# Fewer, larger copies of constant rows between two on-chip tiles, in a gated cross-attention and expert kernel

## The reference

```
x = x + tanh(g_xattn) * attention(layernorm(x), ctx, ctx)   # 16 heads of 8, scores + mask row + window mask
x = x + tanh(g_ffn) * experts(layernorm(x))                 # top 2 of 8 experts, silu(x w1) * (x w3) -> w2
```

## Time and profile before

| | |
|---|---|
| three runs | 480.2, 482.2, 482.57 us (median 482.2) |
| the profiled execution | 482.57 us, its span 480.9 us |
| PE busy | 417.2 us (87%) |
| DVE busy | 304.4 us (63%) |
| POOL busy | 259.4 us (54%) |
| ACT busy | 233.7 us (49%) |
| mean granted TensorE clock | 0.965 |
| DMA traffic | 46.24 MB, mean 96 GB/s |

### The profile page before, as it was taken

How to read it: one execution, slowest core, us unless ns; L and a number is a source line. 1 busy time by engine, 2 the same in 40 slices (tenths; PEclk the granted TensorE clock), 3 DMA queues, 4 the chain that set the end, 5 groups by cost and what they waited for, 6 DMA issues and landing times.

```text
span 480.9 us, 14461 instructions
## 1 busy us (share of the span) xinstructions
PE 417.2 (87%) x4569; PEld 365.3 (76%) x4570; DVE 304.4 (63%) x833; ACT 233.7 (49%) x504; POOL 259.4 (54%) x318
## 2 busy tenths in 40 slices
PE   1878699998888989889688988999999999999980
PEld 0555478777676767667468888999899999999970
DVE  3986878877887878788657345764444554554520
ACT  3778245666565555555364544443344444444430
POOL 5753603214655373737175566777666465565561
PEclk9989989999999899999889998999999999999995
DMA  8945545455655464667573334433544333333326
GB/s 220 282 102 99 93 78 86 90 82 82 118 80 116 64 120 73 120 167 205 183 211 84 96 50 52 61 52 59 77 69 56 53 50 44 49 44 44 27 23 185
DMA packets 74783, 46.24 MB, mean 96 GB/s; under 512 B 8608, under 2 KB 71490, under 8 KB 74562
## 3 DMA queue, kind: packets, MB, share of 16 engines
q1 hardware_dynamic: 59072, 34.84, 33.4%
q0 software_dynamic: 12272, 8.92, 14.1%
q10 hardware_dynamic: 3392, 1.88, 1.6%
HBM read 18.12 MB, written 14.20 MB: 67 GB/s over the span
## 4 chain that ended last, share of the span: by engine, by line
PE 62%; DVE 13%; issue 7%; ACT 5%; DMA 5%; SPq 3%; POOL 1%; ACTq 1%; DVEq 0%; POOLq 0%
PE ps_scores L1594 23%; PE ps_max_scores L1602 12%; PE ps_max_scores L780 6%; PE ps_values L826 6%; PE ps_scores L812 3%; DVE rsplit L1063 3%; DMA sums_scratch<-yt,xg 3%; PE ps_max_scores L762 3%; PE ps_scores L762 2%; DVE qkf L521 1%; PE ps_values L1586 1%; DMA bk_col<-in_L_xattn_bk_dram 1%; ACT xn L448 1%; SPq L1542 1%; DVE ed L1133 1%
## 5 line engine op out<-in xcount | busy, mean ns | idle before, releaser
L1715 POOL DMA_INDIRECT sums_scratch<-yt,xg x71 | 115.0, 1619 | 69.2 <-DMA sums_scratch<-yt,xg 30.3
L1594 PE MATMUL ps_scores<-xgT,qs 128*128 128x128 f32 x1136 | 141.2, 278 | 5.2 <-ACT xgT L1640 3.9
L1594 PEld LDWEIGHTS ps_scores<-xgT,qs 128*128 128x128 f32 x1136 | 134.0, 194 | 6.9 <-ACT xgT L1640 4.5
L1681 DVE TENSOR_TENSOR qs<-qs,ps_scores 128x512 f32<-128x512 f32 x71 | 48.8, 687 | 90.9 <-PE ps_scores L1594 71.7
L1063 DVE TENSOR_REDUCE rsplit<-ps_max_scores 128x4 f32<-128x512 f32 x128 | 85.2, 687 | 26.2 <-PE ps_max_scores L762 25.3
L1289 POOL DMA_INDIRECT expert_rows_scratch<-xr,pos x64 | 66.4, 1038 | 25.3 <-issue 13.4
L1602 PE MATMUL ps_max_scores<-w_all,qs 128*128 x568 | 75.9, 277 | 2.4 <-ACT yt L1651 1.7
L974 ACT ACTIVATE pT<-ps_scores 128x1024 f32<-128x1024 f32 x64 | 65.2, 1020 | 19.0 <-PE ps_scores L762 19.0
L1602 PEld LDWEIGHTS ps_max_scores<-w_all,qs 128*128 128x128 f32 x568 | 69.0, 192 | 4.3 <-issue 4.2
L1644 ACT ACTIVATE qs<-ps_scores 128x512 f32<-128x512 f32 x71 | 42.4, 597 | 32.3 <-PE ps_scores L1594 32.3
L780 PE MATMUL ps_max_scores<-ks,qs 121*128 121x128 bf16 x512 | 51.5, 227 | 6.4 <-DVE rsplit L1063 3.5
(11 more groups left out here) (187 smaller groups left out, 532.4 us busy)
## 6 DMA issues: line engine op xcount, KB each, us to landing
qs<-w_all SPq DMA_DIRECT2D x96, 64.0 KB
ks<-w_all SPq DMA_DIRECT2D x96, 64.0 KB
w_all<-in_L_ffn_w_dram SPq DMA_DIRECT2D x24, 256.0 KB
xg<-expert_rows_scratch SPq DMA_DIRECT2D x71, 65.0 KB, 1.9
xs<-in_x_dram SPq DMA_DIRECT2D x4, 512.0 KB, 5.3
sums_scratch<-xs SPq DMA_DIRECT2D x8, 256.0 KB, 4.1
sums_scratch<-yt,xg POOLq DMA_INDIRECT x71, 3.3
expert_rows_scratch<-fill SPq DMA_DIRECT2D x16, 65.0 KB
```

The source lines that it names most:

```text
L1594: ins = nc.tensor.matmul(bank[u % 2][:, c * P:(c + 1) * P], w13[:, u % 2, n, c * P:(c + 1) * P], xgT[:], start=True, stop=True)
L1681: nc.vector.tensor_tensor(hidT[:, u % 2], act_s[:, u % 2], ps_b[u % 2], ALU.mult).then_inc(hid_ready, 1)
L1715: pool.indirect_dma_start(out=z_d, out_offset=bass.IndirectOffsetOnAxis(ap=xg_u[:, u, X_IDX:X_IDX + 1], axis=0), in_=yt[:, u % YRING], in_ ...
```

## The change

The spans copied from tile 0 to tile 1 are put together: fewer and larger ones that cover the same rows. `at` is ROWS_K (57) for `qs` and ROWS_K + PARTS (60) for `ks`; the span 121-124 of `ks` is added at L290 as before.

```
-        STAY_ROWS = tuple(tuple((at, at + QUART) for at in WIN_AT) + tuple((at + QUART, at + ROWS_W) for at in WIN_AT)
-                          + ((at, WIN_AT[1]),) for at in (ROWS_K, ROWS_K + PARTS))
-        TILE_COPIES = 2 * 5 + 1
+        STAY_ROWS = tuple(((WIN_AT[0], ROWS_W), (at, WIN_AT[1] + ROWS_W)) for at in (ROWS_K, ROWS_K + PARTS))
+        TILE_COPIES = 2 * 2 + 1
```

## The result

The change makes the kernel slower: 497.67 us median of four runs (496.59 to 498.1) against 482.1 (480.2 to 482.57), a ratio of 1.0327 (95% interval 1.0294 to 1.0359). The forecast was 494.0, with a range of 487 to 508. The profiled execution took 498.06 us, its span 496.3.

A forecast was written before the change was run, and what follows sets the result against it. TensorE, busy 87% of the span, was taken to bound the kernel. 482.57 + 10.3 (late first L780) + 1.5 (clock) = 494.4 us; with the median 0.4 lower, the forecast was 494.0, range 487 to 508.

The forecast's parts named there:

- Six issues fewer: SyncE's copies cut from 11 issues to 5: group 0's loads could start 6 us earlier, at 25.3 us, worth 0.
- 0.69 us a row: Time for one engine to move a 16 KiB row; the 37 rows then run from 24.9 to 50.4 us.
- 10 x 0.69 = 6.9 us for the rows ahead: Rows of the first three copies on the lone engine before the 37 rows, from near 18 to 24.9 us.
- The queue: SyncE issues two loads during the 37-row copy, the other 11 after it; first L780 comes 10.3 us late.
- 7.0 + 2.4 us behind the copy: After the 37-row copy ends: 7.0 us for 11 load issues, 2.4 us to landing; first half lands at 59.8 us.
- the deep queue: Rival: all 13 loads queue during the copy, leaving one engine's backlog; 5.4 us late at least, 488 us; chance 0.10.
- What is late next: After group 0's first half: group 1's slacks of 9.6 and 10.5 us cover some 4; later stages run as before.
- The clock, 1.5 us: TensorE's granted clock drops after a 10 us wait, slowing its next 3 us of work: 1.5 us, bounds 0 to 2.5.
- The rival of the slow engine: The lone engine takes 1.14 us for every row, TensorE is 31.5 us late, 515 us; chance 0.09.
- The spread copy: Rival: the 37-row copy isn't put on one engine; TensorE still starts at 49.5, time 482.2 us; chance 0.07.

## Why the prediction was right, and where its size was off

*Six issues fewer: worth 0.* Right in the time. With 36 and 1 rows the loads are issued 0.9 us earlier at their start and 2.4 at their end, and the time is the same. The 6 us by which the prediction let the loads start earlier did not appear, as the mask store landed 12.3 us after its issue (11.2 with 36 and 1 rows) instead of 5.5.
*0.69 us a row.* The 37 rows took 25.7 us, and the forecast had 25.5. This is partly luck. A row that is alone takes 0.61 us (27 GB/s), which makes 22.6, and 3.1 us came on top, since single rows took up to 1.4 us while other engines still copied or loads ran (packet records, 28.4 to 36.5 and 52.9 to 54.2 us). The estimate from the 27 GiB/s of the Trainium skill ("DMA: Bandwidth & Descriptors", "Specifications") is 20.9 us for the 37 rows, and not the 21.4 of the prediction; it is nearer to the 22.6 than 25.5 is, and further from the 25.7.

*10 x 0.69 = 6.9 us for the rows ahead.* This is the mis-sized term. They took from 18.15 to 28.45 us: 10.3 us, 1.03 each. This is near the upper bound of 1.14 that I had read from the copies and kept for the rival only. I used one rate for two situations. Ten rows run beside ten other engines and cost what rows cost there; most of the 37 run alone. Behind the 37 stands one row more that I did not count, of the 3-row copy: 1.0 us. So the forecast's end of 50.4 was 4.8 early: 3.4 from the ten rows, 1.0 from the last one, 0.4 from the start and the 37.

*The queue.* Four loads went out and not two, and then the order was as expected. But the 7.0 + 2.4 us behind the copy were made in another way: the last load was issued at 57.70 and landed 6.19 us later, as the engine had a backlog. 13 loads with 16 pieces each on that engine, 208 pieces, took from 55.2 to 63.9 us, 0.042 us a piece. That is near the upper bound that I gave to the deep queue (8.5 us; 104 KiB at 12.9 GB/s are 8.3), and within 1 us of the 9.4 that I took. So this term came out by another mechanism than the one forecast. The engine had work all that time, so the fifth issue's stand of 17.54 us is the wait's sign and not its cause; that is argued from the records, no run took it away alone.

*What is late next: nothing.* Right. No wait for a load stands in TensorE's waits up to 110 us but the first. When the copy was moved behind group 0's loads, those same slacks did not hold.

*The clock, 1.5 us.* From the first L780 to the first score, 14.3 us became 16.3: 2.0 us. The granted clock over that stretch is 0.62 after and 0.79 before:

```profile
49.50:63.80 14.30, 9.94 (x76) 6.68 (x75) 13.06 (x23) 1.78 (x4) 6.99 (x7) 0.79 0.55 95
```

In sum, the forecast had 10.3 + 1.5 = 11.8 us; it was 14.5 + 2.0 - 1.1 (less by the end of the span) = 15.4.

The rival of the slow engine (1.14 us a row for all) had its rate nearly right for the ten rows and wrong for the 37. The deep queue was half right. The spread copy was wrong.

## What to carry to other kernels

Before two DMAs are put together, factor the number of rows: 33, 36 and 40 rows cost nothing here, 29 and 37, which are prime, ran on one engine, at 0.61 us for each 16 KiB row that was alone. Count the rows of every copy that the busiest engine has, the small copies too. A DMA that nobody waits for can still hold up one that somebody does, through the one engine that both use, and another queue does not protect from it if its packets are large. When a rate is taken from a trace, take one for each situation that the transfer will be in, alone and beside others.

## What the runs showed of the hardware

- An engine that served two queues here took a piece from each in turn, although one was 64 times the size of the other. Beside 16 KiB packets, a load of 256-byte pieces advanced by one piece in about 0.63 us and took 11.4 us to land. The Trainium skill has the turns in "DMA: Bandwidth & Descriptors", section "Queues, rings and completion order": an engine drains a whole packet from one ring before it switches. The trace agrees with the turns. That section gives 9 to 17 descriptors as a typical packet; here one 256-byte piece went in each turn.
- An issue stands when the DMAs ahead have too much left: 17.54 us on SyncE's queue, 26.29 us on ScalarE's, where it stopped the engine's computing as well, and TensorE waited 23.9 us for it.
- A lone row of 16 KiB from tile to tile took 0.611 us over and over. While other engines moved rows or loads, the same engine took 1.03 us a row over ten rows, and up to 1.4 us for one.
